# Four layers of cross-attention on 64 batches: other places for the side units, and the transpose of the maxima moved behind the second scores

## The chip, the cores and the metric

The kernel runs on one core of a Trainium2 chip, in float32. The metric is the time of one execution on the device, in microseconds (us). The kernel before was run three times: 2257.44, 2264.24 and 3683.89 us, median 2264.24 us. One more execution was profiled; it took 2264.95 us.

## The reference, cut to what matters

Four layers follow each other. Each one takes x (64 batches, 128 rows, 160 channels = 20 heads of 8) and a context of 77 rows with 256 channels, of which the last 4 are image tokens.

```python
# layers 0 to 2 (plain attention as far as the kernel needs it), and the text branch of layer 3
q = heads(x @ Wq); k = heads(ctx @ Wk); v = heads(ctx @ Wv)
p = softmax(q @ k.T / sqrt(8))          # per head, over the context rows
out = merge(p @ v)
# layer 3 also has an image branch
qsem = l2norm(einsum(probs_text, text_ctx))        # (b, h, s, 256)
sem = einsum('bhse,bne->bhsn', qsem, l2norm(image_ctx))
probs_ip = softmax(q @ k_ip.T / sqrt(8) + 0.5 * sem) * fside
out = out + merge(probs_ip @ v_ip)
# every layer
x = out @ Wo + b + x
```

The kernel never forms qsem: with the Gram matrix of a batch's context (context times its transpose, 77 x 77) it gets the products with the image tokens and the squared norm from the probabilities alone. This is what the "gram waves" below compute.

## The kernel before, in words

**Steps and rounds.** One step works on one pair of batch and layer at each of several stages. In step t the layer is t % 4, and batch and layer follow from t so that four batches at different layers are in flight. The steps run from -10 to 274; steps 20 to 235 stand in a hardware loop of 9 passes with 24 steps each, the others are written out. Four steps finish one batch; this text calls them a round, and its steps "step 0" to "step 3" by t % 4. Layer 3 (the one with the image branch) enters in step 3. Each engine has its own program order, written out by hand in a function `step`; an engine runs its list in order and waits at semaphores.

**The path of one (batch, layer) pair c.** In step c PE makes the first scores (`scores`, into ps_s: rows of x against keys), DVE takes the maximum of every head over them (`top_of`, four reductions). For layers 0 to 2 PE transposes the 128 x 20 maxima (`turn_top`, L802), ACT copies the result from PSUM to `top_t` (`tops`, L1012), and SP issues four DMAs (`move_top`, L584) that put the maxima as extra rows into `q_sb`. In step c+1 PE makes the scores a second time in transposed form, with the maxima subtracted by those extra rows (`second`, which is `exponents`, L771; it waits for `top_ready`, the landing of the four DMAs), and ACT takes their exponential (`exps`, four instructions, one for each PSUM bank). For layer 3, DVE subtracts the maxima (`less_top`), ACT takes the exponentials (`text_exps`), and `second` is `turn`, 14 transposes (L788) without DMAs. In step c+2 PE multiplies with the values (`product`, L816) and turns the result back (`turn_back`, L852), DVE divides by the sums (`results`). In step c+3 PE turns and projects (`turn_out`, `project_out`, `project_rest`), DVE adds bias and old x (`new_x`).

So layers 0, 1 and 2 need one `move_top` each in a round: that of step 0 is needed by `second` of step 1, that of step 1 by `second` of step 2, that of step 2 by `second` of step 3.

**The side units.** All of these use one PSUM bank, `ps_k`, one after the other, and each waits until the one before has been read out: the keys of a layer for two batches (`keys`, L644, 4 matmuls, read out by ACT), the values of a batch for all layers (`values` and `values_rest`, L670 and L681, read out by ACT), the Gram matrix (`image`, L694, read out by DVE), the image tokens of six batches (`image_tokens`, once in 24 steps), and the four gram waves of a batch (`gram_wave`, L839 and L844; DVE multiplies each by the probabilities, `weigh`, L1171). Three waves are of 6 heads and one is of 2 heads. A wave waits for the `weigh` of the wave before.

**The order of SP.** SP issues all DMAs of the loop: in step 0 `next_x` (3), `move_top` (4), `place_values` (4, L567), `place_gram` (4, L577); in step 1 `move_top` (4); in step 2 `next_context`, `share_values`, `move_top` (4); in step 3 `store` (3). In one step 1 out of six, `save_values` (L546) stands ahead of `move_top`.

**The order of PE in a step** is: scores, turn_out, queries of the next step, values, product, project_out, image, wave 0 (step 1), keys (step 2), image tokens, turn_top, second, wave 0 (step 2), turn_back, wave 1, keys (step 0), values_rest.

Of the kernel before, what the change touches and what calls it, by code (L numbers as in the profile page):

```python
# [11 lines left out]
L = 4  # L12
# [32 lines left out]
CX = 128 + 128 + H * NIP  # L45
VN = TRI * 2 * D
VL = TRI * UC

# [96 lines left out]
def values_batch(t):  # L147
    return (t + 1) // 4 if t % 4 == 3 else -1


def keys_at(t):


    if t % 8 == 4:
        return 0, (t + 4) // 8
    if t % 8 == 2:
        return 1, (t - 2) // 8
    if t % 8 == 6:
        return 2, (t - 6) // 8
    if t % 8 == 0:  # L160
        return 3, (t - 8) // 8
    return 0, -1
# [63 lines left out]
def build(nc, a):  # L226

    ctx = ExitStack()
    with ctx:
# [384 lines left out]
        def _(pe):  # L614
            def units_done(k, t):


                if k is None or t % 4 == 3:
                    pe.wait_ge(vb_evac, raised(k, e_values, t))
                    pe.wait_ge(g_evac, raised(k, e_gram, t))  # L620
                if k is None or t % 4 == 0:
                    pe.wait_ge(six_evac, raised(k, e_six, t))
                    pe.wait_ge(k_evac, raised(k, e_keys, t))
                if k is None or t % 4 in (1, 2):
                    pe.wait_ge(w_ready, raised(k, e_waves, t, per=2))
                if k is None:
                    pe.wait_ge(six_evac, raised(k, e_six, t))
                    pe.wait_ge(k_evac, raised(k, e_keys, t))

            def keys(k, t):  # L630

# [16 lines left out]
            def image_tokens(k, t):  # L648
# [11 lines left out]
                                    wvip[:, kt * C:(kt + 1) * C], start=kt == 0, stop=kt == 1)  # L660
                ins.then_inc(six_psum, 1)

            def values(k, t):


                b = values_batch(t)
                units_done(k, t - 1)
                w = wv[:, :].rearrange("p (l k a n) -> p l k a n", l=L, k=2, a=2)
                for kt in range(2):
                    ins = pe.matmul(ps_k[0:T, 0:L * VN].rearrange("p (l n) -> p l n", l=L), cx(b, kt, 0, T),  # L670
                                    w[:, :, 0, kt, :], start=kt == 0, stop=kt == 1)
                ins.then_inc(v_psum, 1)

            def values_rest(k, t):


                b = values_batch(t)
                pe.wait_ge(va_evac, raised(k, e_values, t))
                w = wv[:, :].rearrange("p (l k a g i d) -> p l k a g i d", l=L, k=2, a=2, g=TRI, i=2)
                for kt in range(2):  # L680
                    ins = pe.matmul(ps_k[0:T, 0:L * TRI * D].rearrange("p (l g d) -> p l g d", l=L, g=TRI),  # L681
                                    cx(b, kt, 0, T), w[:, :, 1, kt, :, 1, :], start=kt == 0, stop=kt == 1)
                ins.then_inc(vb_psum, 1)

            def image(k, t):

                b = gram_batch(t)
                if e_values(t):
                    pe.wait_ge(va_evac, raised(k, e_values, t))
                else:  # L690
                    units_done(k, t - 1)
                at = L * TRI * D
                for kt in range(2):
                    ins = pe.matmul(ps_k[0:T, at:at + T], cx(b, kt, 0, T), cx(b, kt, 0, T),  # L694
                                    start=kt == 0, stop=kt == 1)
                ins.then_inc(g_psum, 1)
# [124 lines left out]
            def gram_wave(k, t, i):  # L821

                c = wave_step(t)
                z = 2 * (t % 4 - 1) + i
                b = batch(c)
                if i == 0:
                    pe.wait_ge(g_ready[b % NX], loads(k, b, NX, per=4))
                    pe.wait_ge(p_ready, raised(k, exists, c, per=4))
                    if e_keys(t):
                        pe.wait_ge(k_evac, raised(k, e_keys, t))  # L830
                    else:
                        units_done(k, t - 1)
                else:
                    pe.wait_ge(w_ready, raised(k, e_waves, t - 1, per=2, more=1))
                for j in range(groups_in(z)):
# [60 lines left out]
            def step(k, t):  # L896
# [9 lines left out]
                    queries(k, t + 1)  # L906
                if ip(out_step(t)):
                    turn_out(k, t)
                if e_values(t):
                    values(k, t)  # L910
                if exists(t - 2):
                    product(k, t - 2)
                if out(t):
                    project_out(k, t)
                    if not topped(t - 1):
                        project_rest(k, t, 0)
                        project_rest(k, t, 1)
                if e_gram(t):
                    image(k, t)
                if e_waves(t) and t % 4 == 1:  # L920
                    gram_wave(k, t, 0)
                if e_keys(t) and t % 4 == 2:
                    keys(k, t)
                if e_six(t):
                    image_tokens(k, t)
                if topped(t):
                    turn_top(k, t)
                if exists(t - 1):
                    second(k, t - 1)
                if e_waves(t) and t % 4 == 2:  # L930
                    gram_wave(k, t, 0)
                if exists(t - 2):
                    turn_back(k, t - 2)
                if e_waves(t):
                    gram_wave(k, t, 1)
                if e_keys(t) and t % 4 == 0:
                    keys(k, t)
                if e_values(t):
                    values_rest(k, t)

# [7 lines left out]
        def _(act):  # L948
# [33 lines left out]
            def values(k, t):  # L982
                b = values_batch(t)
                act.wait_ge(v_psum, raised(k, e_values, t))
                if b > 0:
                    act.wait_ge(v_ready[(b - 1) % NC], loads(k, b - 1, NC, per=4))
                for i in range(2):
                    ins = act.activation(v_img[i][:, :].rearrange("p (g u) -> p g u", u=UC)[:, :, i * D:(i + 1) * D],
                                         ps_k[0:T, 0:L * VN].rearrange("p (g u) -> p g u", u=2 * D)
                                         [:, :, i * D:(i + 1) * D], ACT.Copy)  # L990
                ins.then_inc(va_evac, 1)

            def values_rest(k, t):
                act.wait_ge(vb_psum, raised(k, e_values, t))
                if e_gram(t):
                    act.wait_ge(g_psum, raised(k, e_gram, t))
                act.activation(v_img[2][:, :].rearrange("p (g u) -> p g u", u=UC)[:, :, 2 * D:3 * D],
                               ps_k[0:T, 0:L * TRI * D].rearrange("p (g u) -> p g u", u=D), ACT.Copy)\
                   .then_inc(vb_evac, 1)

            def queries(k, c):
                act.wait_ge(q_psum, raised(k, exists, c))
# [54 lines left out]
            def step(k, t):  # L1057
# [3 lines left out]
                    results(k, t)  # L1061
                if exists(t + 1):
                    queries(k, t + 1)
                if e_values(t):
                    values(k, t)
                if exists(t - 2):
                    products(k, t - 2)
                if e_keys(t) and t % 4 == 2:
                    keys(k, t)
                if e_six(t):  # L1070
                    image_tokens(k, t)
                if topped(t):
                    tops(k, t)
                if ip(t):
                    for i in range(4):
                        text_exps(k, t, i)
                for i in range(2):
                    if exists(t - 1):
                        exps(k, t - 1, i)
                if ip(t - 6):  # L1080
                    image_exp(k, t - 6)
                for i in range(2, 4):
                    if exists(t - 1):
                        exps(k, t - 1, i)
                if e_keys(t) and t % 4 == 0:
                    keys(k, t)
                if e_values(t):
                    values_rest(k, t)

            run(act, step)  # L1090

        @block.vector
        def _(dve):
# [56 lines left out]
            def image(k, t):  # L1150
# [4 lines left out]
                    dve.wait_ge(vb_evac, raised(k, e_values, t))  # L1155
                if b > 0:
                    dve.wait_ge(g_ready[(b - 1) % NX], loads(k, b - 1, NX, per=4))
                at = L * TRI * D
                dve.tensor_tensor(g_img[:, T:2 * T], ps_k[0:T, at:at + T], mask_g[:, :], ALU.mult)
                dve.tensor_tensor(w_img[:, T:2 * T], ps_k[0:CUT, at:at + T], mask_w[:, :], ALU.mult).then_inc(g_evac, 1)  # L1160

            def weigh(k, t, i):

                c = wave_step(t)
                z = 2 * (t % 4 - 1) + i
                lo, hi = BH * z, BH * z + heads_in(z)
                if i == 0:
                    dve.wait_ge(p_marked, raised(k, ip, c))
# [119 lines left out]
            def step(k, t):  # L1288
                for i in range(4):
                    if exists(t):  # L1290
                        top_of(k, t, i)
                        if ip(t):
                            less_top(k, t, i)
                if e_waves(t) and t % 4 == 1:
                    weigh(k, t, 0)
                if ip(t - 5):
                    norms(k, t - 5)
                    image_branch(k, t - 5, 1, 8)
                if ip(t - 6):
                    image_branch(k, t - 6, 16, 19)  # L1300
                if out(t):
                    new_x(k, t)
                if e_waves(t) and t % 4 == 2:
                    weigh(k, t, 0)
                if ip(t - 6):
                    image_branch(k, t - 6, 19, 21)
                    image_weights(k, t - 6)
                if exists(t - 2):
                    results(k, t - 2)
                if e_waves(t):  # L1310
                    weigh(k, t, 1)
                if ip(t - 5):
                    image_branch(k, t - 5, 8, 16)
                if e_gram(t):
                    image(k, t)

# [183 lines left out]
```

## Time and profile before

| | |
|---|---|
| median of three runs | 2264.24 us |
| profiled execution, own time | 2264.95 us |
| its span, first to last instruction | 2263.2 us |
| mean granted TensorE clock | 0.970 |
| PE, busy share | 92% |
| DVE, busy share | 65% |
| ACT, busy share | 48% |
| POOL, busy share | 20% |

PE is TensorE (matmuls), PEld its weight loads, DVE is VectorE, ACT ScalarE, POOL GpSimd, SP the engine that issues DMAs (SPq in the rows). One float32 matmul shows as two records, so x28 is 14 matmuls. Times in the rows count from the start of the span.

### The profile page before, as it was taken

The page shows a single profiled execution, that of the slowest core. Times are in us where ns is not written, and L with a number is a line of the kernel's source. Part 1 is how long each engine was busy: PE and PEld are TensorE (multiplying, and loading weights), DVE is VectorE, ACT ScalarE, POOL GpSimd, SP SyncE. Part 2 cuts the span into 40 slices and gives each one's busy share as a digit, 9 for nine tenths or more (in the row PEclk, how much of TensorE's full clock was granted, in tenths as well). Part 3 has the DMA queues.
Part 4 walks back from the last instruction along what each step waited for, and adds up shares of the span by engine and source line. Part 5 has one row for each costly group of instructions (what it writes and reads, how often), then busy time and mean ns, then how long its engine had stood idle before and what let it go on. Part 6 is the DMA issues. An engine that isn't in the chain of part 4 may idle for free.

```text
span 2263.2 us, 75842 instructions
## 1 busy us (share of the span) xinstructions
PE 2086.4 (92%) x26394; PEld 1697.5 (75%) x26394; DVE 1481.7 (65%) x4449; ACT 1075.1 (48%) x2733; POOL 458.7 (20%) x870
## 2 busy tenths in 40 slices
PE   2699999999999999999999999999999999999975
PEld 1567877887787788778778877887887788778764
DVE  3236776777677676767767766776676677667654
ACT  0245554455445455544545554554554455555431
POOL 0112122212212221221222122122212222222110
PEclk9889999999999999999999999999999999999975
DMA  3111111211111121112111111211211121111000
GB/s 82 49 43 50 52 43 42 52 50 39 47 52 44 41 52 51 38 46 52 45 41 52 52 38 47 53 44 40 52 52 38 47 53 44 39 53 38 22 10 5
DMA packets 108576, 101.31 MB, mean 45 GB/s; under 512 B 42240, under 2 KB 84952, under 8 KB 108184
## 3 DMA queue, kind: packets, MB, share of 16 engines
q1 hardware_dynamic: 104556, 92.88, 15.1%
q8 instruction: 231, 3.78, 0.7%
q10 hardware_dynamic: 3628, 3.33, 0.6%
q14 instruction: 161, 1.32, 0.2%
HBM read 34.13 MB, written 5.41 MB: 17 GB/s over the span
## 4 chain that ended last, share of the span: by engine, by line
PE 78%; SPq 8%; DVE 5%; issue 4%; DMA 2%; ACT 2%; ACTq 1%; DVEq 0%; POOLq 0%; POOL 0%
PE ps_s L738 11%; PE ps_c L816 10%; PE ps_s L771 8%; PE ps_c L886 6%; PE ps_k L839 6%; PE ps_k L644 5%; PE ps_q L717 5%; PE ps_c L875 4%; PE ps_k L670 4%; PE ps_s L788 4%; PE ps_k L844 4%; SPq L584 3%; PE ps_c L891 3%; PE ps_c L852 2%; SPq L577 2%
## 5 line engine op out<-in xcount | busy, mean ns | idle before, releaser
L1131 DVE TENSOR_REDUCE top<-ps_s 128x6 f32<-128x462 f32 (+3 forms) x1024 | 511.3, 546 | 88.2 <-PE ps_s L738 84.3
L1027 ACT ACTIVATE p_t<-ps_s 116x512 f32<-116x512 f32 (+1 forms) x768 | 372.9, 545 | 48.9 <-PE ps_s L771 46.9
L738 PE MATMUL ps_s<-k_blocks,q_sb 32*128 32x231 f32 (+1 forms) x3584 | 347.8, 384 | 20.3 <-issue 18.5
L816 PE MATMUL ps_c<-p_t,v_rows 116*27 116x128 f32 (+1 forms) x7168 | 288.7, 284 | 14.8 <-DMA v_rows<-v_img 12.3
L738 PEld LDWEIGHTS ps_s<-k_blocks,q_sb 32*128 32x128 f32 x3584 | 229.9, 185 | 84.9 <-issue 31.3
L816 PEld LDWEIGHTS ps_c<-p_t,v_rows 116*27 116x27 f32 (+1 forms) x7168 | 214.1, 108 | 86.5 <-issue 49.3
L1055 ACT ACTIVATE o_t<-ps_c 128x256 f32<-128x256 f32 x256 | 98.1, 383 | 368.3 <-PE ps_c L875 302.7
L1354 POOL TENSOR_TENSOR k_blocks<-k_sb,mask_k 128x231 f32<-128x231 f32 x384 | 211.8, 573 | 267.6 <-PE ps_s L771 252.5
L771 PE MATMUL ps_s<-q_sb,k_blocks 32*116 32x128 f32 (+1 forms) x5376 | 223.8, 283 | 27.7 <-DMA q_sb<-top_t 15.0
L839 PE MATMUL ps_k<-gram,p_t 116*128 116x154 f32 x896 | 210.6, 317 | 41.6 <-DVE weighted L1171 41.6
L771 PEld LDWEIGHTS ps_s<-q_sb,k_blocks 32*116 32x116 f32 (+1 forms) x5376 | 186.3, 175 | 63.7 <-issue 52.0
L1363 POOL TENSOR_TENSOR weighted<-weighted 128x720 f32<-128x720 f32 x64 | 93.0, 1453 | 679.3 <-DVE weighted L1171 679.3
L1171 DVE TENSOR_TENSOR weighted<-ps_k,probs 128x462 f32<-128x462 f32 (+1 forms) x256 | 142.6, 557 | 118.2 <-PE ps_k L844 118.2
L644 PE MATMUL ps_k<-context,wk 128*128 128x154 f32 (+1 forms) x1024 | 159.4, 299 | 40.8 <-DVE minus L1122 40.2
L886 PE MATMUL ps_c<-o_t,wo_lead 128*128 128x128 f32 x1024 | 185.8, 305 | 2.4 <-ACT o_t L1055 2.4
L839 PEld LDWEIGHTS ps_k<-gram,p_t 116*128 116x128 f32 x896 | 137.2, 193 | 66.4 <-DVE weighted L1171 57.9
L886 PEld LDWEIGHTS ps_c<-o_t,wo_lead 128*128 128x128 f32 x1024 | 136.7, 194 | 56.1 <-issue 52.1
L1282 DVE SCALAR_TENSOR_TENSOR x_out<-ps_c,bias,x_work 128x128 f32<-128x128 f32 x64 | 22.5, 351 | 234.9 <-PE ps_c L891 234.9
L644 PEld LDWEIGHTS ps_k<-context,wk 128*128 128x128 f32 x1024 | 142.5, 194 | 42.9 <-issue 42.9
L1040 ACT ACTIVATE u_sb<-ps_c 128x256 f32<-128x256 f32 x256 | 98.1, 383 | 160.9 <-PE ps_c L816 160.9
L844 PE MATMUL ps_k<-gram,p_t 115*128 115x115 f32 (+1 forms) x896 | 166.1, 266 | 0.0
L891 PE MATMUL ps_c<-o_t,wo_tail 32*128 32x128 f32 x1024 | 164.3, 280 | 0.0
(118 smaller groups left out, 3595.3 us busy)
## 6 DMA issues: line engine op xcount, KB each, us to landing
v_rows<-v_img SPq DMA_DIRECT2D x128, 227.4 KB
context<-in_ctx SPq DMA_DIRECT2D x64, 336.0 KB, 3.0
q_sb<-top_t SPq DMA_DIRECT2D x576, 6.0 KB
v_rows<-v_img SPq DMA_DIRECT2D x64, 115.2 KB
v_rows<-v_img SPq DMA_DIRECT2D x64, 112.2 KB
v_rep<-v_dram SPq DMA_DIRECT2D x64, 50.0 KB
q_sb<-top_t SPq DMA_DIRECT2D x192, 2.0 KB
gram<-g_img SPq DMA_DIRECT2D x64, 46.3 KB
```

Of the source, the lines that this page charges most:

```text
L644: ins = pe.matmul(o[:, :, 0:n], w_rows(wk, l, kt, m, 128), cx_pair(p, kt, 0, n), start=kt == 0, stop=kt == 1)
L738: ins = pe.matmul(ps_s[:, z * 512 + j * GT:z * 512 + j * GT + n], q_sb[c % 3][lo:lo + QUAD, j * S:(j + 1) * S], k_blocks[c % 3][lo:lo + QU ...
L771: ins = pe.matmul(ps_s[0:n, to:to + S], k_blocks[c % 3][lo:lo + QUAD, col:col + n], q_sb[c % 3][lo:lo + QUAD, j * S:(j + 1) * S], start=Tr ...
L816: ins = pe.matmul(ps_c[t % 2][32 * (g % 4):32 * (g % 4) + UC, g // 4 * S:(g // 4 + 1) * S], v_rows[b % NC][0:n, v:v + UC], p_t[c % 3][0:n, ...
L839: pe.matmul(ps_k[:, to:to + 2 * T], p_t[c % 3][0:n, at:at + S], gram[b % NX][0:n, 0:2 * T], start=j == 0, stop=False, skip_group_check=True)
L844: ins = pe.matmul(ps_k[:, to:to + m], p_t[c % 3][0:n, at:at + S], gram[b % NX][0:n, 2 * T:2 * T + m], start=False, stop=True, skip_group_c ...
L886: pe.matmul(ps_c[(t - LAG) % 2][:, j * S:(j + 1) * S], o_rows(wo_lead, l, j), o_t[:, 0:S], start=j == 0, stop=False, skip_group_check=True)
L891: ins = pe.matmul(ps_c[(t - LAG) % 2][:, j * S:(j + 1) * S], o_rows(wo_tail, l, j)[TAIL:LEAD, :], o_t[TAIL:LEAD, S:2 * S], start=False, st ...
L1027: act.activation(to, source, ACT.Exp, scale=SCALE).then_inc(p_ready, 1)
L1131: dve.tensor_reduce(top[c % 2][:, z * BH:z * BH + m], s.rearrange("p (h t) -> p h t", t=T)[:, :, 0:n], AX.X, ALU.max).then_inc(s_top, 1)
L1171: dve.tensor_tensor(weighted[:, lo * T:hi * T], ps_k[:, 0:(hi - lo) * T], probs[:, lo * T:hi * T], ALU.mult).then_inc(w_ready, 1)
L1354: pool.tensor_tensor(k_blocks[c % 3][:, j * GT:(j + 1) * GT].rearrange("p (h t) -> p h t", t=T), keys_of(l, b // 2)[:, at:at + T].unsqueez ...
```

## The change

The change gives several units new places in the order of each engine. The matrix shapes of keys, waves and Gram matrix stay.

- **Keys**: those that stood in step 2, ahead of `turn_top`, now stand in step 3, behind `turn_out` and ahead of `product`. Those of step 0 stay at its end.
- **Values**: they are cut in two units of two layers each, where one unit had all layers for two of three head groups and the second the rest. Each unit is now 4 matmuls (two of 224 columns, two of 112) in place of 2 of 448 columns and 2 of 224. ACT reads each unit out with 3 instructions (before: 2 and 1). The first unit stands behind `project_out` in step 3, the second at the end.
- **Image** (the Gram matrix) goes behind `turn_back` in step 3.
- **Gram waves**: both steps 1 and 2 have their wave 0 ahead of `second`, and the order of the waves becomes banks 3, 0, 1, 2, so that the short wave is the first and not the last.
- **The maxima**: on PE `turn_top` goes from ahead of `second` to behind it. On ACT `tops` goes from ahead of `exps` to between the second and the third of the four. SP's order is untouched.
- **ACT**: `image_exp` goes from the middle of `exps` to behind `queries`; the last of four `text_exps` goes to the end of the step.
- **DVE**: `new_x`, `weigh`, `results` and the 20 small instructions of the image branch get another order. Steps 8 to 18 of the branch now all run in step 0 (steps 16 to 18 stood in step 1), and steps 8 to 13 stand ahead of `results` there.

```diff
@@ PE, step
                 if ip(out_step(t)):
                     turn_out(k, t)
-                if e_values(t):
-                    values(k, t)
+                if e_keys(t) and t % 4 == 3:
+                    keys(k, t)
                 if exists(t - 2):
                     product(k, t - 2)
...
-                if e_gram(t):
-                    image(k, t)
-                if e_waves(t) and t % 4 == 1:
+                if e_values(t):
+                    values(k, t)
+                if e_waves(t):
                     gram_wave(k, t, 0)
-                if e_keys(t) and t % 4 == 2:
-                    keys(k, t)
                 if e_six(t):
                     image_tokens(k, t)
+                if exists(t - 1):
+                    second(k, t - 1)
                 if topped(t):
                     turn_top(k, t)
-                if exists(t - 1):
-                    second(k, t - 1)
-                if e_waves(t) and t % 4 == 2:
-                    gram_wave(k, t, 0)
                 if exists(t - 2):
                     turn_back(k, t - 2)
                 if e_waves(t):
                     gram_wave(k, t, 1)
                 if e_keys(t) and t % 4 == 0:
                     keys(k, t)
+                if e_gram(t):
+                    image(k, t)
                 if e_values(t):
                     values_rest(k, t)
@@ PE, gram_wave
-                z = 2 * (t % 4 - 1) + i
+                z = BANKS[2 * (t % 4 - 1) + i]
@@ ACT, step
+                if ip(t - 6):
+                    image_exp(k, t - 6)
+                if e_keys(t) and t % 4 == 3:
+                    keys(k, t)
+                if exists(t - 2):
+                    products(k, t - 2)
                 if e_values(t):
                     values(k, t)
...
+                if ip(t):
+                    for i in range(3):
+                        text_exps(k, t, i)
+                if exists(t - 1):
+                    for i in range(2):
+                        exps(k, t - 1, i)
                 if topped(t):
                     tops(k, t)
...
+                if exists(t - 1):
+                    for i in range(2, 4):
                         exps(k, t - 1, i)
@@ DVE, step
-                if e_waves(t) and t % 4 == 1:
+                if ip(t - 6):
+                    image_branch(k, t - 6, 19, 21)
+                    image_weights(k, t - 6)
+                if e_waves(t):
                     weigh(k, t, 0)
                 if ip(t - 5):
                     norms(k, t - 5)
                     image_branch(k, t - 5, 1, 8)
...
+                if ip(t - 5):
+                    image_branch(k, t - 5, 8, 14)
                 if exists(t - 2):
                     results(k, t - 2)
+                if out(t) and ip(out_step(t)):
+                    new_x(k, t)
                 if e_waves(t):
                     weigh(k, t, 1)
                 if ip(t - 5):
-                    image_branch(k, t - 5, 8, 16)
+                    image_branch(k, t - 5, 14, 19)
```

## Rows read from the trace of the kernel before

**Rows 1.** The page: the span, the busy time of PE, the chain that ended last.

```profile
span 2263.2 us, 75842 instructions
...
PE 2086.4 (92%) x26394; PEld 1697.5 (75%) x26394; DVE 1481.7 (65%) x4449; ACT 1075.1 (48%) x2733; POOL 458.7 (20%) x870
...
PE 78%; SPq 8%; DVE 5%; issue 4%; DMA 2%; ACT 2%; ACTq 1%; DVEq 0%; POOLq 0%; POOL 0%
```

**Rows 2.** Waits, steps 20 to 235: total us, times, longest us.

```profile
PE ps_k L839 <- DVE weighted L1171: 31.5, 53, 0.6
...
PE ps_s L738 <- issue: 18.5, 8, 2.5
...
PE ps_s L771 <- DMA q_sb<-top_t: 8.8, 14, 1.1
```

**Rows 3.** Timeline of PE, one round from second of step 0 on: start us, us.

```profile
1220.16 0.28 PE L802 MATMUL ps_q<-ident,top 128*20 128x128 f32 x1
1220.28 1.69 PE L788 MATMUL ps_s<-ident,probs 128*116 128x128 f32 x14
1221.81 0.38 PE L852 MATMUL ps_c<-ident,u_sb 128*128 128x128 f32 x2
...
1226.47 0.43 PE L839 MATMUL ps_k<-gram,p_t 116*128 116x154 f32 x2
...
1227.43 0.27 PE L802 MATMUL ps_q<-ident,top 128*20 128x128 f32 x1
1227.64 0.81 PE L771 MATMUL ps_s<-q_sb,k_blocks 32*116 32x128 f32 x19
...
1234.61 1.21 PE L644 MATMUL ps_k<-context,wk 128*128 128x154 f32 x8
1235.66 0.27 PE L802 MATMUL ps_q<-ident,top 128*20 128x128 f32 x1
1235.87 0.81 PE L771 MATMUL ps_s<-q_sb,k_blocks 32*116 32x128 f32 x19
...
1239.01 0.53 PE L839 MATMUL ps_k<-gram,p_t 116*128 116x154 f32 x2 [0.61 <-DVE weighted L1171]
...
1241.33 1.67 PE L670 MATMUL ps_k<-wv,context 128*77 128x448 f32 x4
```

**Rows 4.** Timeline of PE: second of step 0 in the next round.

```profile
1252.01 1.69 PE L788 MATMUL ps_s<-ident,probs 128*116 128x128 f32 x14
```

**Rows 5.** Timeline of SP in the round of Rows 3: DMA issues.

```profile
1220.77 3.07 SPq L584 DMA_DIRECT2D q_sb<-top_t  x4
1223.89 3.20 SPq L567 DMA_DIRECT2D v_rows<-v_img  x4
1227.21 0.78 SPq L577 DMA_DIRECT2D gram<-g_img  x1
1228.03 1.49 SPq L577 DMA_DIRECT2D gram<-w_img  x1
1229.56 1.50 SPq L577 DMA_DIRECT2D gram<-g_img  x2
1231.18 3.12 SPq L584 DMA_DIRECT2D q_sb<-top_t  x4
```

**Rows 6.** The chain of waits in a round with a late second of step 2.

```profile
1134.55 1.72 DMA q_sb<-top_t
1136.27 0.23 issue
1136.49 1.03 PE ps_s L771 x19
```

**Rows 7.** Timeline of SP in the round of Rows 6.

```profile
1121.02 3.10 SPq L584 DMA_DIRECT2D q_sb<-top_t  x4
...
1132.12 3.11 SPq L584 DMA_DIRECT2D q_sb<-top_t  x4
```

**Rows 8.** Timeline of DVE in the round of Rows 3.

```profile
1224.83 1.96 DVE L1131 TENSOR_REDUCE top<-ps_s 128x2 f32<-128x154 f32 x4
...
1228.46 0.24 DVE L1252 TENSOR_REDUCE f_top<-fused 128x20 f32<-128x80 f32 x1
```

**Rows 9.** Busy times by stretch around a loop end; PEclk is the granted clock.

```profile
388.70:390.80 2.10, 0.01 (x1) 0.00 (x0) 0.77 (x4) 0.88 (x3) 0.11 (x1) 1.00 0.17 45
391.40:394.80 3.40, 3.40 (x38) 2.88 (x35) 1.75 (x4) 0.77 (x2) 0.00 (x0) 0.50 0.02 5
```

More of the change, by code:

```diff
@@ L47 @@
 VL = TRI * UC
+VU = 2 * (VN + TRI * D)
 LEAD = 128
@@ L155, in keys_at @@
         return 0, (t + 4) // 8
[L156 to L159, printed above, removed]
+    if t % 8 == 3:
+        return 1, (t - 3) // 8
+    if t % 8 == 7:
+        return 2, (t - 7) // 8
     if t % 8 == 0:
@@ L626, in units_done @@
                 if k is None:
+                    pe.wait_ge(k_evac, raised(k, e_keys, t))
                     pe.wait_ge(six_evac, raised(k, e_six, t))
-                    pe.wait_ge(k_evac, raised(k, e_keys, t))
             def keys(k, t):
@@ L661, in image_tokens, with values_unit @@
                 ins.then_inc(six_psum, 1)
-            def values(k, t):
[L666 to L672, printed above, removed]
+            def values_unit(b, u):
+                w = wv[:, :].rearrange("p (l k a n) -> p l k a n", l=L, k=2, a=2)[:, 2 * u:2 * u + 2]
+                third = w.rearrange("p l k a (g i d) -> p l k a g i d", g=TRI, i=2)
+                for kt in range(2):
+                    pe.matmul(ps_k[0:T, 0:2 * VN].rearrange("p (l n) -> p l n", l=2), cx(b, kt, 0, T),
+                              w[:, :, 0, kt, :], start=kt == 0, stop=kt == 1)
+                for kt in range(2):
+                    ins = pe.matmul(ps_k[0:T, 2 * VN:VU].rearrange("p (l g d) -> p l g d", l=2, g=TRI),
+                                    cx(b, kt, 0, T), third[:, :, 1, kt, :, 1, :], start=kt == 0, stop=kt == 1)
+                return ins
+            def values(k, t):
+                if e_keys(t):
+                    pe.wait_ge(k_evac, raised(k, e_keys, t))
+                else:
+                    units_done(k, t - 1)
+                values_unit(values_batch(t), 0).then_inc(v_psum, 1)
             def values_rest(k, t):
-                b = values_batch(t)
                 pe.wait_ge(va_evac, raised(k, e_values, t))
[L679 to L683, printed above, removed]
+                values_unit(values_batch(t), 1).then_inc(vb_psum, 1)
             def image(k, t):
@@ L691, in image @@
                     units_done(k, t - 1)
-                at = L * TRI * D
+                at = VU
                 for kt in range(2):
@@ L828, in gram_wave @@
                     pe.wait_ge(p_ready, raised(k, exists, c, per=4))
[L829 to L832, printed above, removed]
+                    units_done(k, t - 1)
                 else:
@@ L986, in values, with values_out @@
                     act.wait_ge(v_ready[(b - 1) % NC], loads(k, b - 1, NC, per=4))
[L987 to L991, printed above, removed]
+                values_out(0).then_inc(va_evac, 1)
+            def values_out(u):
+                for i in range(GH):
+                    to = v_img[i][:, 2 * u * VL:2 * (u + 1) * VL].rearrange("p (g u) -> p g u", u=UC)
+                    if i < 2:
+                        source = ps_k[0:T, 0:2 * VN].rearrange("p (g u) -> p g u", u=2 * D)[:, :, i * D:(i + 1) * D]
+                    else:
+                        source = ps_k[0:T, 2 * VN:VU].rearrange("p (g u) -> p g u", u=D)
+                    ins = act.activation(to[:, :, i * D:(i + 1) * D], source, ACT.Copy)
+                return ins
             def values_rest(k, t):
@@ L996, in values_rest @@
                     act.wait_ge(g_psum, raised(k, e_gram, t))
-                act.activation(v_img[2][:, :].rearrange("p (g u) -> p g u", u=UC)[:, :, 2 * D:3 * D],
-                               ps_k[0:T, 0:L * TRI * D].rearrange("p (g u) -> p g u", u=D), ACT.Copy)\
-                   .then_inc(vb_evac, 1)
+                values_out(1).then_inc(vb_evac, 1)
             def queries(k, c):
@@ L1063, in step @@
                     queries(k, t + 1)
+                if ip(t - 6):
[4 more added lines that the diff above has]
+                    products(k, t - 2)
                 if e_values(t):
                     values(k, t)
[L1066 to L1069, printed above, removed]
                 if e_six(t):
                     image_tokens(k, t)
+                if ip(t):
[4 more added lines that the diff above has]
+                        exps(k, t - 1, i)
                 if topped(t):
                     tops(k, t)
[L1074 to L1083, printed above, removed]
+                if exists(t - 1):
+                    for i in range(2, 4):
                         exps(k, t - 1, i)
@@ L1088, in step @@
                     values_rest(k, t)
+                if ip(t):
+                    text_exps(k, t, 3)
             run(act, step)
@@ L1157, in image @@
                     dve.wait_ge(g_ready[(b - 1) % NX], loads(k, b - 1, NX, per=4))
-                at = L * TRI * D
+                at = VU
                 dve.tensor_tensor(g_img[:, T:2 * T], ps_k[0:T, at:at + T], mask_g[:, :], ALU.mult)
@@ L1164, in weigh @@
                 c = wave_step(t)
-                z = 2 * (t % 4 - 1) + i
+                z = BANKS[2 * (t % 4 - 1) + i]
                 lo, hi = BH * z, BH * z + heads_in(z)
@@ L1298, in step @@
                     image_branch(k, t - 5, 1, 8)
-                if ip(t - 6):
-                    image_branch(k, t - 6, 16, 19)
-                if out(t):
+                if out(t) and not ip(out_step(t)):
                     new_x(k, t)
[L1303 to L1307, printed above, removed]
+                if ip(t - 5):
+                    image_branch(k, t - 5, 8, 14)
                 if exists(t - 2):
                     results(k, t - 2)
+                if out(t) and ip(out_step(t)):
+                    new_x(k, t)
                 if e_waves(t):
```

## The prediction

> **What bounds the kernel now.** I read the page first. PE is busy for 92% of the span, and the chain that ended last is 78% PE, but 8% of it is SP issuing DMAs [rows 1]. So PE nearly bounds the kernel, and something on SP now and then bounds it instead. The view of waits, cut to the loop, names what PE still waits for: 31.5 us in 53 equal pieces of 0.6 us for the `weigh` between two gram waves, 18.5 us in 8 pieces at the jumps of the loop, and 8.8 us in 14 pieces for the DMAs that move the maxima [rows 2]. The first is one per round. The third shows that the way of the maxima has hardly any reserve, and the timelines tell how much.
>
> Call A0, A1, A2 the starts of `second` in steps 0, 1 and 2. In the round shown they are 1220.28, 1227.64 and 1235.87, and the next A0 is 1252.01 [rows 3, 4]. A round is 31.73 us; without the 0.61 us wait it is 31.12 us of PE streaming. Now SP in the same round [rows 5]: the four copies of the maxima of step 0 are issued from 1220.77 on, then without a pause the eight copies of values and Gram matrix, then the four copies of step 1, which end at 1231.18 + 3.12 = 1234.30. One DMA issue costs SP about 0.8 us, so these sixteen cost 13.53 us. In a round where PE did wait, the last issue ended at 1132.12 + 3.11 = 1135.23, the copy had landed at 1134.55 + 1.72 = 1136.27, which is 1.04 us later, and PE started 0.23 us after that [rows 6, 7]. Put on the quiet round: 1234.30 + 1.04 + 0.23 = 1235.57, and A2 is 1235.87. The reserve is 0.30 us. This is the number on which the change turns: from A0 to A2 PE needs 15.59 us and the maxima's way through SP needs 15.29 us.
>
> **The change part by part.**
>
> **Gram waves.** With wave 0 of step 2 ahead of `second`, the whole of `second`, from 1235.87 on in the row, lies between the two waves of that step, longer than the 0.61 us that PE waits now. That wait goes [rows 3]: -0.61 us a round. In step 1 `second` lay between its waves already. The short wave is now the first; the waves' total on PE is the same. POOL's `fold` waits for the last `weigh`, which is now a long one, some 0.3 us later; its result is wanted by the `norms` of the next step 0, a whole step later, so this is hidden.
>
> **Values.** 672 columns twice over, before and after. The two matmuls of 448 columns took 1.67 us, 0.83 us each, which is 0.21 us for 112 columns. A 128 column matmul, the turn of the maxima, holds PE for 0.21 us as well [rows 3]. So a matmul of 112 columns costs about its columns, and the four extra matmuls can cost from 0 (weight loads hidden) to 0.8 us (none of it hidden). I take +0.1 us, since the turn of the maxima is the nearest row. ACT gets three more instructions, and the keys, in step 3, ahead of the exponentials that `scores` of step 0 waits for. It is 48% busy [rows 1]. This can cost from 0 to one instruction's time in a round; I take 0, because PE's own step 3 grows by the 1.05 us of the keys and pushes that need back.
>
> **Keys.** 1.05 us of PE (1234.61 to 1235.66) go from ahead of A2 into step 3 [rows 3]. Total nothing. But A0 to A2 becomes shorter.
>
> **PE's way from A0 to A2 after the change.** 15.59, less 1.05 (keys), plus 0.96 (a long wave now ahead of A2; one took from 1226.47 to 1227.43), less 0.48 (half a wave, since the short one replaces a long one in step 1), less 0.21 and plus 0.21 (`turn_top` leaves the front of A2 and enters behind A0): 15.02 us.
>
> **The maxima.** `turn_top` of step 0 started 0.12 us ahead of A0. Now it can start when the 14 transposes have streamed, 1221.81 - 1220.28 = 1.53 us behind A0: 1.65 us later [rows 3]. ACT's two exponentials ahead of the copy need banks 3 and 0, which the 14 transposes fill first, so I add nothing for them (0 to about 0.6 us, if one were still running). SP waits at that `move_top`, and behind it in its queue stand the eight copies and then the four of step 1. All sixteen start 1.65 us later. Nobody wants the eight early, but `second` of step 2 wants the last four. The way of the maxima becomes 15.29 + 1.65 = 16.94 us against PE's 15.02: PE stands idle ahead of A2 for 1.92 us in every round. For step 1 itself SP starts 1.53 + 0.61 = 2.14 us behind A0 (the turn started at 1220.16, SP at 1220.77), and the way is 2.14 + 3.07 + 1.04 + 0.23 = 6.5 us against 7.36 - 0.48 = 6.9 on PE: it still fits, barely. For the copies of step 2, SP has only two other issues ahead, and PE's step 3 grows by the keys; I see no wait there.
>
> **DVE.** Three more branch instructions (one took 0.24 us, with its gap 0.27) now stand ahead of the maxima of step 1, which therefore end at 1226.79 + 0.8 = 7.3 us behind A0, while PE is at A1 after 6.9 [rows 3, 8]. So A1 may slip by up to 0.4 us. The cover is the idle time at A2: SP's queue does not depend on A1, so it costs nothing while the 1.92 us stand, and 0.4 us a round if they don't.
>
> **Sum.** -0.61 + 0.1 + 1.92 = +1.41 us for a quiet round. In the one round of six with `save_values` the first `move_top` was late already by about half a microsecond, so it shifts less: about +1.2. In the rounds that waited a little already the reserve of 0.30 is absent: about +1.7. The mean is 1.4. Of 64 rounds the first and the last few idle anyway; I count 60: +85 us. On the profiled execution's 2264.95 us that is 2350 us, and that execution stands 0.7 us above the median.
>
> **The rivals.**
>
> *The way of the maxima is no bound.* If SP's sixteen issues took 1.9 us less than in the rows, or if the first copy could go earlier, PE would find the maxima landed at A2. Then only the gain is left: -0.61 + 0.1 = -0.5 us a round, 60 rounds, and 2235 us, 1.3% under before. For it: the loop's 54 rounds show only 14 waits there [rows 2]. Against it: SP's queue shows no pause between the first and the last of the sixteen, and the reserve is 0.30 us. It decides at a lateness of 0.87 us (0.30 + 0.57); below that the change gains.
>
> *The idle time lowers the clock.* At the loop's jump PE stood still for 2.1 us at full clock and then ran 3.40 us at a granted clock of 0.50, that is 1.2 GHz [rows 9]. The idle of 1.9 us at A2 is close to that, and PE's longest wait for these DMAs in the loop was 1.1 us [rows 2]. The Trainium skill, "TensorE: Matmul & The Clock Gate", says the same in its part on the clock gate: the throttled state is the default and activity releases it. 3.4 us at half the clock cost between 0 and 1.7 us of streaming; I take 1.0, since small matmuls don't double. Sixty more microseconds: 2410 us.
>
> **How the numbers follow.** The forecast has a chance of 0.68; with idle times from 1.2 to 2.4 us at A2 it spans 2307 to 2380 us. The clock case has 0.16, the first rival 0.16. The range from 2285 to 2412 takes in the forecast, the clock and half of the way down to the rival, and leaves that rival out. A change within 2% is about what a measurement of this kernel can't tell from none; 2% above the median is 2309.5. Slower by over 2%: nearly all of the forecast and the clock case, 0.79. Within 2%: 0.18. Faster by over 2%: 0.03; the whole gain that I can find is 1.3%.
>
> **What would show it.** In the profile after: PE's waits for the DMAs `q_sb<-top_t` at L771 should be near 2 us each, one per round, 100 us or more in all. The wait of L839 for `weighted` should be gone. SP should show sixteen issues without a pause that begin 2.1 us behind A0. The four issues of step 2 should cause no wait. A round should be 33.1 us. If there is no wait at L771 the forecast is wrong; if the granted clock falls once a round behind A2, the second rival holds.

## The result and the profile after

The kernel after takes 2368.82 us (median of 4 runs, 2364.42 to 2378.39); the kernel before, on the same chip, 2265.95 us. The ratio is 1.0468, with a 95% interval of 1.0437 to 1.0499: slower by 4.7%, 103 us. One of the four executions of the kernel before took 3683.89 us; the ratio leaves it out. Forecast were 2350 us and a range of 2285 to 2412. The profiled execution took 2378.39 us, the longest of the four, with a span of 2376.3 us.

The page of the kernel after, as in [rows 1]:

```profile
span 2376.3 us, 77049 instructions
...
PE 2139.6 (90%) x26906; PEld 1838.5 (77%) x26906; DVE 1504.6 (63%) x4449; ACT 1069.7 (45%) x2925; POOL 459.7 (19%) x870
```

PE lost two points of share while the span grew by 113 us. Its busy time grew too, by 53 us. A part of that is in the clock and a part in `second`, which holds PE longer; both are measured below. The four added matmuls of a round take none of it that shows: the two units of values hold PE for 1.23 us each, 2.46 us together, where they held it for 1.60 and 0.85 us, 2.45 together. What PE waits for in the loop answers to [rows 2]:

```profile
PE ps_s L776 <- DMA q_sb<-top_t: 76.9, 52, 2.4
...
PE ps_c L877 <- DVE o_sb L1198: 16.0, 42, 1.3
PE ps_s L743 <- issue: 15.5, 8, 2.2
```

The wait of the gram waves for `weigh`, 31.5 us in 53 pieces before, is gone. In its place stands one wait per round for the DMAs that move the maxima, 1.5 us in the mean where 14 short ones stood. That is 76.9 us in all, where the prediction looked for 100 or more. A second one is new: `turn_out` waits for DVE's `o_sb` in 42 of the 54 rounds. A third is small: `product` waits for the copies of the values, 7.1 us in 18 pieces. One round on PE, as in [rows 3, 4] (start us, us):

```profile
1088.93 1.74 PE L793 MATMUL ps_s<-ident,probs 128*116 128x128 f32 x14
...
1090.51 0.27 PE L807 MATMUL ps_q<-ident,top 128*20 128x128 f32 x1
...
1090.84 1.16 PE L645 MATMUL ps_k<-context,wk 128*128 128x146 f32 x8
...
1093.62 0.44 PE L877 MATMUL ps_c<-ident,o_sb 128*128 128x128 f32 x2 [0.47 <-DVE o_sb L1198]
...
1096.49 1.05 PE L776 MATMUL ps_s<-q_sb,k_blocks 32*116 32x128 f32 x21
...
1097.90 0.28 PE L807 MATMUL ps_q<-ident,top 128*20 128x128 f32 x1
...
1106.07 1.13 PE L776 MATMUL ps_s<-q_sb,k_blocks 32*116 32x128 f32 x22 [1.33 <-DMA q_sb<-top_t]
...
1107.47 0.28 PE L807 MATMUL ps_q<-ident,top 128*20 128x128 f32 x1
...
1122.51 1.75 PE L793 MATMUL ps_s<-ident,probs 128*116 128x128 f32 x14
```

A0, A1, A2 and the next A0 are 1088.93, 1096.49, 1106.07 and 1122.51. The round is 33.58 us (31.73 before; forecast 33.1). A0 to A2 is 17.14 us (15.59 before; forecast 16.94), and PE stands still for 1.33 us ahead of A2. SP in the same round, as in [rows 5]:

```profile
1091.11 3.07 SPq L585 DMA_DIRECT2D q_sb<-top_t  x4
1094.22 3.20 SPq L568 DMA_DIRECT2D v_rows<-v_img  x4
1097.54 0.78 SPq L578 DMA_DIRECT2D gram<-g_img  x1
1098.37 1.56 SPq L578 DMA_DIRECT2D gram<-w_img  x1
1099.97 1.50 SPq L578 DMA_DIRECT2D gram<-g_img  x2
1101.60 3.20 SPq L585 DMA_DIRECT2D q_sb<-top_t  x4
```

The sixteen issues begin 1091.11 - 1088.93 = 2.18 us behind A0 (forecast 2.14) and run without a pause to 1104.80. Another 1.27 us later PE starts, the same landing and start as in [rows 6, 7]. The way of the maxima, not PE, sets A2.

### The profile page after: what moved, and what is told of

Its sections match the earlier page's. It is cut to its first block and busy times, and to the rows that moved or that the text cites. A ratio compares the mean times of both kernels' runs of the same rounds, so it can differ in the third digit from the quotient of the medians.

```text
span 2376.3 us, 77049 instructions
## 1 busy us (share of the span) xinstructions
PE 2139.6 (90%) x26906; PEld 1838.5 (77%) x26906; DVE 1504.6 (63%) x4449; ACT 1069.7 (45%) x2925; POOL 459.7 (19%) x870
## 5 line engine op out<-in xcount | busy, mean ns | idle before, releaser
L1031 ACT ACTIVATE p_t<-ps_s 116x512 f32<-116x512 f32 (+1 forms) x768 | 367.5, 537 | 348.3 <-PE ps_s L776 347.8
L743 PE MATMUL ps_s<-k_blocks,q_sb 32*128 32x231 f32 (+1 forms) x3584 | 364.0, 389 | 16.5 <-issue 15.5
L776 PE MATMUL ps_s<-q_sb,k_blocks 32*116 32x128 f32 (+1 forms) x5376 | 257.2, 295 | 109.1 <-DMA q_sb<-top_t 93.1
L776 PEld LDWEIGHTS ps_s<-q_sb,k_blocks 32*116 32x116 f32 (+1 forms) x5376 | 216.7, 183 | 134.0 <-issue 105.7
L743 PEld LDWEIGHTS ps_s<-k_blocks,q_sb 32*128 32x128 f32 x3584 | 253.3, 190 | 64.9 <-issue 26.7
L821 PE MATMUL ps_c<-p_t,v_rows 116*27 116x128 f32 (+1 forms) x7168 | 282.8, 280 | 22.8 <-DMA v_rows<-v_img 19.9
L1190 DVE RECIPROCAL recip<-ps_c 128x21 f32<-128x21 f32 x256 | 75.7, 296 | 237.7 <-PE ps_c L854 232.1
L846 PE MATMUL ps_k<-gram,p_t 115*128 115x115 f32 (+1 forms) x896 | 172.2, 274 | 0.0
L1029 ACT ACTIVATE p_t<-ps_s 116x512 f32<-116x512 f32 (+1 forms) x256 | 128.7, 530 | 69.4 <-PE ps_s L793 66.6
```

The lines of the kernel that those rows point to most:

```text
L743: ins = pe.matmul(ps_s[:, z * 512 + j * GT:z * 512 + j * GT + n], q_sb[c % 3][lo:lo + QUAD, j * S:(j + 1) * S], k_blocks[c % 3][lo:lo + QU ...
L776: ins = pe.matmul(ps_s[0:n, to:to + S], k_blocks[c % 3][lo:lo + QUAD, col:col + n], q_sb[c % 3][lo:lo + QUAD, j * S:(j + 1) * S], start=Tr ...
L821: ins = pe.matmul(ps_c[t % 2][32 * (g % 4):32 * (g % 4) + UC, g // 4 * S:(g // 4 + 1) * S], v_rows[b % NC][0:n, v:v + UC], p_t[c % 3][0:n, ...
L846: ins = pe.matmul(ps_k[:, to:to + m], p_t[c % 3][0:n, at:at + S], gram[b % NX][0:n, 2 * T:2 * T + m], start=False, stop=True, skip_group_c ...
L1031: act.activation(to, source, ACT.Exp, scale=SCALE).then_inc(p_ready, 1)
```

## The experiments

Each kernel was timed next to the kernel before on the same chip. Ratios are to that.

| run | median us | ratio, 95% interval |
|---|---|---|
| units alone, maxima at the old place | 2282.33 | 1.0077, 1.0048 to 1.0105 |
| maxima alone, units at the old places | 2355.05 | 1.0387, 1.0354 to 1.0420 |
| maxima moved in step 0 alone | 2364.54 | 1.0425, 1.0392 to 1.0459 |
| maxima moved in steps 1 and 2 alone | 2267.07 | 1.0026, 1.0006 to 1.0045 |
| after, Gram copies one step later | 2242.19 | 0.9897, 0.9869 to 0.9925 |
| units alone, Gram copies one step later | 2246.84 | 0.9922, 0.9894 to 0.9950 |
| before, Gram copies one step later | 2235.20 | 0.9872, 0.9850 to 0.9894 |
| after, filler on PE | 2366.64 | 1.0451, 1.0431 to 1.0471 |
| after, better DVE order | 2364.86 | 1.0446, 1.0409 to 1.0483 |
| after, Gram later, results first | 2248.31 | 0.9927, 0.9903 to 0.9951 |
| after, Gram later, better DVE order | 2249.38 | 0.9926, 0.9899 to 0.9952 |
| the same, maxima at the old place | 2221.78 | 0.9822, 0.9788 to 0.9856 |

**The two halves of the change.** The units alone:

```diff
 # the kernel after, PE (and ACT likewise: tops ahead of the exponentials)
+                if topped(t):
+                    turn_top(k, t)
                 if exists(t - 1):
                     second(k, t - 1)
-                if topped(t):
-                    turn_top(k, t)
```

> The kernel after, with turn_top and tops back at the places of before (ahead of second, ahead of the exponentials); all units at their new places. If the late maxima in SP's queue are the cause, the wait of L776 for the maxima is gone and only the gain is left: about -0.5 us a round, 2235 us. If the new places of the units (DVE and ACT in steps 3, 0 and 1) are the cause, it stays over 2320 us.

Measured: 2282.33 us, neither. The maxima's place carries most of the cost, but the units did not gain; they lost 0.8%. The waits say where (units alone, loop, 53 of its 54 rounds):

```profile
PE ps_c L877 <- DVE o_sb L1198: 25.2, 43, 1.0
PE ps_q L807 <- DVE top L1137: 19.6, 48, 0.9
PE ps_s L776 <- DMA q_sb<-top_t: 17.0, 18, 1.6
```

The first DVE row is in step 1, and the second too but for four of its pieces. Steps 8 to 13 of the image branch now stand ahead of `results` in step 0, so `o_sb` is late for `turn_out`; steps 14 to 18 stand ahead of the maxima of step 1, so these are late too. Together 44.8 us, 0.85 us a round, more than the 0.61 us that the waves give back. The wait for the maxima's DMAs has grown as well, from 8.8 us [rows 2] to 17.0. Less the 31.5 us of the waves, and 3.9 us less at the loop's jumps, all this makes 17.6 us more waiting, against 16.8 us by which the median is longer.

The maxima alone, in the kernel before:

```diff
 # PE (and ACT likewise: tops between the second and third exps)
-                if topped(t):
-                    turn_top(k, t)
                 if exists(t - 1):
                     second(k, t - 1)
+                if topped(t):
+                    turn_top(k, t)
```

> The kernel before with turn_top moved behind second and tops moved between two exponentials; the units stay. By the queue theory all sixteen issues of SP start 1.65 us later against a reserve of 0.30 us: 1.35 us a round, 2345 us, with up to 30 us more if the idle time lowers the clock in some rounds. If the units are the cause, 2265 us.

Measured: 2355.05 us, as the queue theory had it (2345, and up to 30 more for the clock). Moving one small transpose and one small copy costs 90 us.

**Which of the three turns costs.** The same edit under a condition on the step: in the first kernel only where `t % 4 == 0`, in the second only elsewhere.

> The kernel before with turn_top and tops at the new place in step 0 alone. By the queue theory this one carries the whole cost, since the sixteen issues start with it: 1.35 us a round as with all three moved, 2340 to 2355 us. If each of the three late turns costs by itself, a third of the cost: 2295 us.

> The kernel before with turn_top and tops at the new place in steps 1 and 2 alone. By the queue theory SP is still busy with the copies of values and Gram matrix when the maxima of step 1 come, and those of step 2 have reserve: no cost, 2260 to 2272 us. If each late turn costs by itself, two thirds: 2325 us.

Measured: 2364.54 and 2267.07 us. The first is 10 us above its range; its trace has the granted clock at 0.50 for 75 us of the loop, against 44 us with all three turns moved. The turn of step 0 carries all of the cost, the other two carry 0.3%. The waits of L771 for the maxima in the loop, first step 0 alone (51 of its 54 rounds):

```profile
PE ps_s L771 <- DMA q_sb<-top_t: 60.5, 51, 2.2
```

and steps 1 and 2 alone:

```profile
PE ps_s L771 <- DMA q_sb<-top_t: 9.4, 19, 1.3
```

In the first kernel the wait is at `second` of step 2, for the maxima of step 1, though only the turn of step 0 was moved: in one round A0 is at 1001.63, A1 at 1009.33 without a wait, and A2 at 1018.74 behind an idle time of 1.12 us. So the delay travels through SP's queue and not along the data.

**What stands between them in SP's queue.**

```diff
 # the kernel after, SP, behind move_top and place_values
-                if e_gram(t - 1):
-                    place_gram(k, t - 1)
+                if e_gram(t - 2):
+                    place_gram(k, t - 2)
```

> The kernel after, with the four copies of the Gram matrix issued one step later on SP, behind move_top of step 1. By the queue theory 4 us leave the way from the first maxima to the last, which then has about 2 us of reserve: no wait at A2, 2235 to 2255 us. If the copies of the maxima are late by themselves (the turn, ACT's copy, the landing) and not by what stands between them, it stays at 2350 us or more.

Measured: 2242.19 us. One edit on SP takes off 127 us and turns the kernel after from 4.7% slower into 1.0% faster than before. That is not yet a gain of the change: what the same edit does for the kernel before stands below. SP in one round of this kernel:

```profile
1085.93 3.08 SPq L585 DMA_DIRECT2D q_sb<-top_t  x4
1089.05 3.20 SPq L568 DMA_DIRECT2D v_rows<-v_img  x4
1093.15 3.12 SPq L585 DMA_DIRECT2D q_sb<-top_t  x4
1096.32 0.83 SPq L578 DMA_DIRECT2D gram<-g_img  x1
```

and PE at A0 and A2 of that round:

```profile
1083.75 1.74 PE L793 MATMUL ps_s<-ident,probs 128*116 128x128 f32 x14
...
1099.23 0.81 PE L776 MATMUL ps_s<-q_sb,k_blocks 32*116 32x128 f32 x19
```

SP again starts 2.18 us behind A0, so the maxima are as late as in the kernel after. But there is now a pause in front of the second four (1092.25 to 1093.15), they end at 1096.27, and A0 to A2 is 15.48 us with no wait for them. With the 1.27 us from the last issue to PE's start they would allow A2 at 1097.54, so the reserve is 1.69 us.

The same edit on the units alone and on the kernel before:

> Both: maxima at their places of before, units at the new ones, copies of the Gram matrix one step later. By the queue theory the rounds that still waited a little lose that too: 2225 to 2235 us, the least of the four. If SP's queue does not matter, equal to the kernel with the units alone.

> The kernel before with the four copies of the Gram matrix issued one step later, behind move_top of step 1. By the queue theory the quiet rounds had a reserve of 0.30 us and gain nothing, only the 14 waits of the loop (8.8 us) and a few in the last rounds go: 2248 to 2258 us. If SP's queue cost more than its waits show, under 2240 us.

Measured: 2246.84 and 2235.20 us. The first is above its range of 2225 to 2235; the two waits for DVE are still there, 43.1 us in the loop. The second is below its range: the way through SP had cost the kernel before 30 us, not the 7 to 17 that I gave it. Its waits in the loop were 8.8 us [rows 2] and are gone. Of the 30 us, 19 are gained in the loop's 54 rounds and 10 behind them; what makes up the part of the 19 that shows as no wait was not taken apart.

With the Gram copies later in both, the kernel after takes 0.9897 of the kernel before as it was and the kernel before 0.9872, with intervals that overlap (2242.19 and 2235.20 us). So without the queue the change neither gains nor costs anything that can be told from the spread.

**The clock.** In the kernel after:

```diff
+                if t % 4 == 2 and exists(t - 1):
+                    bank_read(k, t, 0)
+                    for i in range(5):
+                        pe.transpose(ps_s[:, 0:S], ident[:, :], ident[:, :])
                 if exists(t - 1):
                     second(k, t - 1)
```

> The kernel after with 5 more 128x128 transposes of the identity on PE ahead of second of step 2, about 1.05 us of work that nobody uses, into a part of ps_s that second overwrites. They fit into the idle time before A2. If that idle time lowers the granted clock in some rounds, those falls go and the kernel with more work is faster: about 2350 us. If the clock plays no part, 2368 us or up to 10 more.

Measured: 2366.64 us against 2368.82 (the intervals overlap): no gain that can be told from the spread. But the clock does fall behind some of the long waits. The timeline of the kernel after has, in one of the rounds with `save_values`,

```profile
1002.84 1.58 PE L776 MATMUL ps_s<-q_sb,k_blocks 32*116 32x128 f32 x21 [2.28 <-DMA q_sb<-top_t]
```

and the busy times by stretch, columns as in [rows 9]:

```profile
1003.20:1006.40 3.20, 3.20 (x37) 2.97 (x36) 0.36 (x2) 1.81 (x5) 0.00 (x0) 0.50 0.33 105
1006.50:1012.00 5.50, 5.50 (x72) 4.75 (x72) 5.22 (x13) 1.97 (x5) 3.27 (x5) 0.99 0.08 19
```

After an idle time of 2.28 us PE ran for over 3 us at 0.50, which is 1.2 GHz, and then at full clock. Behind the 1.33 us of the quiet round above it stayed at 1.00. So the clock falls in some rounds. The Trainium skill, "TensorE: Matmul & The Clock Gate", says in its part on the clock gate that the idle state is the throttled one; the row agrees. The length of the wait alone does not decide: falls stand behind waits of 1.43 to 2.44 us at `second`, and behind other waits of up to 2.04 us there is none.

The traces give the size. In the loop of the profiled execution of the kernel after, the clock is at 0.50 for 78.5 us in 20 stretches, 17 of them at a wait of `second`; before it is 27.3 us in 8 stretches, all at the loop's jumps. A fall costs 1.3 us: of two rounds at the same place in a pass of the loop, one with a fall, for 3.4 us, takes 17.69 us from A2 to the next A0 (from 1418.00 on) and one without takes 16.36 (from 1836.49 on). Scaled to the 51 us more at 0.50, that is about 20 us of this execution (an estimate). It was the longest of the four, with a mean granted clock of 0.955; the others had 0.960 to 0.962 and must have lost less. With the filler the clock is at 0.50 for 30.7 us, in 9 stretches, 7 of them at the jumps, so in this execution (mean clock 0.974; the others 0.964 to 0.970) the filler took nearly all the falls at `second` away. Its time hides a part of that, for PE also stood still for 25.6 us at the 8 jumps, where it was 15.5. So the clock's part of the 103 us is some ten or twenty us, not the sixty of the rival and not nothing.

**DVE's order.** In the kernel after, `results` goes ahead of steps 8 to 13, steps 16 to 18 of the branch go behind the maxima of step 1, and ACT's `image_exp` goes behind `products`:

```diff
                 if ip(t - 6):
+                    image_branch(k, t - 6, 16, 19)
                     image_branch(k, t - 6, 19, 21)
...
+                if exists(t - 2):
+                    results(k, t - 2)
                 if ip(t - 5):
                     image_branch(k, t - 5, 8, 14)
-                if exists(t - 2):
-                    results(k, t - 2)
...
-                    image_branch(k, t - 5, 14, 19)
+                    image_branch(k, t - 5, 14, 16)
```

> The kernel after with DVE's image branch in a better order: results ahead of steps 8 to 13, steps 16 to 18 behind the maxima of step 1 (and ACT's image_exp behind products). With the units alone this order cost PE about 0.98 us a round in step 1. By the queue theory A2 waits for SP and not for this, so nothing is gained: 2360 to 2372 us. If the DVE order is a part of the cost of the change, 50 us less, near 2320 us.

Measured: 2364.86 us, nothing gained. As long as SP sets A2, the lateness of DVE in step 1 is under its cover; the waits for the maxima's DMAs are 77.3 us there, as in the kernel after. With the Gram copies one step later that cover is gone; `results` alone moved, then the whole order, then the whole order with the maxima at the old place:

> The kernel after with the Gram copies one step later and results ahead of steps 8 to 13 of the branch. The wait of turn_out for o_sb (0.6 us a round) goes, but second of step 1 then waits for the maxima of step 1 instead: 2230 to 2242 us, little against 2242.

> The kernel after with the Gram copies one step later and DVE's whole better order. SP's queue is now in time, so the DVE order counts: a quiet round of 31.1 us in place of 31.7, 2242 - 30 = 2212 us (2205 to 2220). If DVE's order does not matter, 2242 us.

> The same with turn_top and tops at their places of before. With SP and DVE both in time the place of the maxima should not matter: 2205 to 2220 us, equal to the run with the new place within 5 us.

Measured: 2248.31, 2249.38 and 2221.78 us. All three miss their ranges. In the first the wait for `o_sb` went, and `second` of step 1 grew instead: it holds PE for 1.78 us in the mean of the loop, where it was 1.34 with the Gram copies later alone. In the second nothing was gained either against 2242.19 us (ratio 0.9926 against 0.9897). A new wait took the place of that for `o_sb` (whole order, maxima at the new place, loop):

```profile
PE ps_k L841 <- DVE weighted L1177: 36.6, 53, 1.0
PE ps_s L743 <- issue: 14.0, 8, 2.0
```

The second wave of step 1 waits for `weigh` of the first, which DVE now does behind the maxima and five branch steps. With the maxima at the old place the same wait is short (53 of the 54 rounds):

```profile
PE ps_s L743 <- issue: 14.4, 8, 2.2
PE ps_k L841 <- DVE weighted L1177: 6.8, 16, 0.6
```

and this kernel is the fastest of all, 1.8% under the kernel before (interval 1.4 to 2.1%). Of that, 1.3% are the Gram copies alone; the units and DVE's order add about 0.5%, with intervals that just touch. So my view that the place of the maxima would not matter any more was wrong by 28 us. Why the wait shrinks with the old place was not taken apart.

## Why the prediction was right

**The mechanism.** It was the one named: all sixteen issues of SP begin later and `second` of step 2 wants the last four. The kernels with the turn moved in step 0 alone and in steps 1 and 2 alone, and the one with four of the sixteen issues taken out of the way, show it from both sides. In the rounds with `save_values` the forecast was +1.2 us; a pair of them went from 16.48 to 17.67 us between A0 and A2, +1.19.

**Its size.** The way of the maxima was forecast at 16.94 us and is 17.14: SP's start was off by 0.04, its issues took 13.69 in place of 13.53. PE's idle time at A2 was forecast at 1.92 us and is 1.33 in the quiet round, because PE's own way took 15.81 us where I had 15.02. Two things in step 1, which I had as a slip of up to 0.4 under the same cover, are as large as these 0.79 us: 0.47 us of waiting for `o_sb`, and 0.32 us in `second` of step 1, which lasts 1.41 us to the next unit (1096.49 to 1097.90) where it was 1.09. The other differences on the way are small and cancel. A1 came 7.56 us behind A0 where I had 6.9. DVE's last maxima of step 1 ended at 1096.70, 7.77 us behind A0 where I had 7.3, so `second` had begun before them; that its later banks waited for them is read from the program and was not tried.

**The gram waves.** -0.61 us a round: the wait is gone in the kernel after. Right, but on its own it would not have been kept: the units alone are slower than before.

**The values.** The four extra matmuls cost 0.01 us on PE: the two units last 1.23 us each (1113.55 to 1114.78, and again from 1116.42), 1.60 us (1241.33 to 1242.93) and 0.85 us (1214.49 to 1215.34) before; 0.1 us was taken.

**The DVE step was mis-sized.** "Up to 0.4 us a round" measured 0.85 us when SP did not hide it. It named the late maxima alone (0.37 us of it); the wait for `o_sb` behind the branch steps that now stand ahead of `results` was not foreseen. It did not change the total, for the reason given there. But it changes the first rival: with the maxima no bound, the kernel after takes 2242 us or more, and against the kernel before with the same relief, 2235, the gain of 1.3% is not there.

**The sum.** 60 rounds of 1.42 us gave 85 us; measured are 103. The round shown is 1.85 us longer than before: 1.55 from A0 to A2 (forecast 1.35) and 0.30 from A2 to the next A0 (forecast about zero). I had no term for the second part. It is in `second` of step 2 itself: behind the wait it holds PE for 1.40 us to the next unit (1106.07 to 1107.47), where it was 1.08 in the kernel before (1235.87 to 1236.95) and is 1.09 with the Gram copies later, where nothing is waited for (1099.23 to 1100.32). In 31 of the loop's 54 rounds the clock stays at 1.00 in both traces; there the mean is +1.61 us, of which 0.18 stand behind A2, for in some of these rounds `second` had waited before too. Over all 54 rounds the mean is +1.92; the difference, some 17 us, is for the most part the clock's (an estimate), which the sum had at nothing. Then the ends of the program: the first A0 comes 12.3 us later than before (180.81 against 168.48), the round ahead of the loop takes 3.0 us more, and 5.8 us are gained again behind the loop. These 9.5 us are near the 8.5 that the sum had for its six rounds outside the loop, but by luck: most of them pass ahead of the first A0, where it had counted nothing. All this adds up to the 113 us of the profiled execution; the median is 10 us less.

**The rivals.** The first, in which the maxima arrive in time, is what the Gram copies one step later bring about. Its limit of 0.87 us does not come out of the prediction's own terms. PE's way to A2 shrinks by 0.57 us, so the reserve of 0.30 us shrinks too and is not added to: at a lateness of 1.65 us the idle time is 1.92, and the change gains only while the idle time is under 0.51 us, which is a lateness under 0.24 us. The second, the clock, is real in single rounds, at about a third or less of the sixty us that it was given.

## What to carry to other kernels

A step on the data path that ends in a queue of issues delays all that stands behind it in the queue. Before moving it, find who waits for the last entry and what reserve it has: here 0.30 us for a move that was forecast at 1.65 us and measured 1.69 (SP began 0.49 us behind A0 before and 2.18 after). Here the cheaper cure was in the queue: copies that nobody wants soon went behind those that somebody waits for. Give that cure to the kernel before as well, or the change is credited with what the cure did. Waits that hide under a larger one show no price until the larger one is gone, and come out one after the other.

## What the runs showed of the hardware that was not expected

SP's one issue of a Gram copy from `w_img` took 1.49 us in the kernel before [rows 5] and 1.56 in the kernel after, where it comes a little behind the issues of the values. It took 0.79 us with the Gram copies one step later, where it stands behind the maxima of step 1:

```profile
1097.18 0.79 SPq L578 DMA_DIRECT2D gram<-w_img  x1
1098.02 1.49 SPq L578 DMA_DIRECT2D gram<-g_img  x2
```

Nor does the slow issue belong to the copy from `w_img`. In a round of the kernel after in which the first Gram copy began 0.04 us behind the values, at 993.60 (0.12 us in the round above), that copy's issue took 1.79 us and the one from `w_img` 0.77 us. So SP's issue time is not a property of the copy alone. What it waits for was not tried.

The same 28 records of `second` in step 2 hold PE for 1.08 or 1.09 us when PE comes to them at work, and for 1.40 us behind a wait for the maxima, at a granted clock of 1.00 (1106.07 to 1109.50). A wait on PE here costs more than its idle time. Why was not tried.
